# Two encoder layers on one core: the transposes of a head pair put in front of the value product of the pair before it

## What is computed

```python
def _L0_attn_ref(x, norm_scale, wq, wk, wv, w_out, b_out):
    h = _rmsnorm(x, norm_scale)
    q = jnp.einsum('bsd,dhe->bshe', h, wq)
    k = jnp.einsum('bsd,dhe->bshe', h, wk)
    v = jnp.einsum('bsd,dhe->bshe', h, wv)
    q = (q * head_dim ** -0.5)
    weights = jnp.einsum('bqhd,bkhd->bhqk', q, k)
    weights = jax.nn.softmax(weights, axis=-1)
    new_vals = jnp.einsum('bhqk,bkhd->bqhd', weights, v)
    return jnp.einsum('bqhe,hed->bqd', new_vals, w_out) + b_out
...
x = _layernorm(x + _L0_attn_ref(x, ...))
x = _layernorm(x + _L0_ffn_ref(x, ...))
x = _layernorm(x + _L1_attn_ref(x, ...))
x = _layernorm(x + _L1_ffn_ref(x, ...))
```

## Time and profile before

| | us |
|---|---|
| median of 3 runs | 1398.1 |
| lowest and highest of them | 1395.76, 1400.56 |
| the profiled execution | 1395.95 |
| its span, first to last instruction | 1394.2 |
| one turn, from OUT of turn 6 to OUT of turn 7 | 82.4 |
| TensorE busy over the span | 1329.1 |
| VectorE busy | 939.4 |
| ScalarE busy | 827.6 |
| GpSimd busy | 501.9 |

### The profile page before, as it was taken

One profiled execution on the slowest core, in us unless ns is written; L12 is line 12 of the kernel. 1 busy time (PEld: TensorE's weight loads), 2 busy tenths in 40 slices (PEclk: granted clock), 3 DMA queues, 4 the chain that ended last, 5 costly groups with the idle time before them and its releaser, 6 DMA issues.

```text
span 1394.2 us, 33724 instructions
## 1 busy us (share of the span) xinstructions
PE 1329.1 (95%) x11200; PEld 1177.8 (84%) x11200; DVE 939.4 (67%) x2663; ACT 827.6 (59%) x2236; POOL 501.9 (36%) x410
## 2 busy tenths in 40 slices
PE   6797999999999999999999999999999999999868
PEld 4575989899898988989898898989889898998758
DVE  5367576675767767676775757677676766757684
ACT  6564755657476574756657575665747556564423
POOL 3407062260705317071441706235070622607000
PEclk9999999999999999999999999999999999999988
DMA  6221000000000000000000000000000000000000
GB/s 186 58 63 33 9 22 12 21 18 12 19 11 23 11 19 11 19 19 8 26 12 15 15 15 23 8 23 15 15 16 14 21 11 20 14 12 21 5 0 9
DMA packets 39392, 30.90 MB, mean 22 GB/s; under 512 B 9897, under 2 KB 37426, under 8 KB 39346
## 3 DMA queue, kind: packets, MB, share of 16 engines
q1 hardware_dynamic: 39346, 30.33, 7.6%
HBM read 27.94 MB, written 2.36 MB: 22 GB/s over the span
## 4 chain that ended last, share of the span: by engine, by line
PE 80%; issue 8%; DVE 3%; POOL 3%; POOLq 2%; DVEq 1%; DMA 1%; SPq 1%; ACT 0%; ACTq 0%
PE bank_F L1222 22%; PE bank_S L1103 7%; PE bank_A L1159 7%; PE bank_T L1136 7%; PE bank_T L1089 4%; PE bank_A L1150 4%; PE bank_T L1090 3%; PE bank_T L1091 3%; PE bank_A L1089 3%; PE bank_F L1089 3%; PE bank_F L1091 3%; PE bank_F L1090 3%; PE bank_A L1091 3%; PE bank_A L1090 3%; POOLq L350 1%
## 5 line engine op out<-in xcount | busy, mean ns | idle before, releaser
L1222 PE MATMUL bank_F<-down,hid 128*128 128x128 f32 x2944 | 357.5, 277 | 5.4 <-DVE x L812 4.7
L1222 PEld LDWEIGHTS bank_F<-down,hid 128*128 128x128 f32 x2944 | 342.1, 193 | 14.4 <-DVE x L812 8.0
L605 ACT ACTIVATE probs<-bank_S,neg_max 128x256 f32<-128x256 f32 x512 | 235.7, 474 | 158.6 <-DVE neg_max L729 158.6
L729 DVE TENSOR_REDUCE neg_max<-bank_S 128x2 f32<-128x512 f32 x256 | 164.5, 684 | 77.2 <-PE bank_S L1103 77.1
L528 POOL TENSOR_TENSOR hid<-hid,qkv 128x1024 f32<-128x1024 f32 x60 | 169.0, 2827 | 11.3 <-ACT hid L621 11.3
L812 DVE SCALAR_TENSOR_TENSOR x<-bank_F,gates,x 128x128 f32<-128x128 f32 x496 | 149.5, 343 | 29.0 <-PE bank_F L1222 20.5
L589 ACT ACTIVATE probsT<-bank_T 128x512 f32<-128x512 f32 x256 | 138.9, 601 | 49.5 <-PE bank_T L1136 49.5
L498 POOL TENSOR_TENSOR mean_sq<-sum_sq,one_over_d 128x2 f32<-128x2 f32 x16 | 3.1, 196 | 429.5 <-ACT h_row L584 429.5
L1159 PE MATMUL bank_A<-probsT,values 128*64 128x256 f32 x1024 | 138.8, 392 | 9.0 <-DVE hid L746 4.1
L516 POOL TENSOR_TENSOR hid<-qkv 128x1024 f32<-128x1024 f32 x45 | 121.1, 2692 | 59.3 <-ACT qkv L589 59.3
L1136 PE MATMUL bank_T<-ident,probs 128*128 128x128 f32 x1024 | 137.5, 277 | 0.1
(11 more groups left out here) (184 smaller groups left out, 2896.3 us busy)
## 6 DMA issues: line engine op xcount, KB each, us to landing
inv_spread<-sums_apart SPq DMA_DIRECT2D x256, 64.0 KB, 2.6
sums_apart<-sum_invT SPq DMA_DIRECT2D x512, 0.5 KB
x_row<-in_x SPq DMA_DIRECT2D x16, 128.0 KB, 2.3
hid<-in_w SPq DMA_DIRECT2D x4, 512.0 KB, 4.5
down<-in_w SPq DMA_DIRECT2D x4, 512.0 KB, 4.4
out<-x SPq DMA_DIRECT2D x16, 128.0 KB, 1.8
hid<-in_rw SPq DMA_DIRECT2D x1, 1024.0 KB, 7.1
hid<-in_wv SPq DMA_DIRECT2D x1, 512.0 KB, 4.0
```

The costliest lines, as they stand in the source:

```text
L605: ins = sc.activation(probs[:, h // 2 % 2, h % 2, t, :], unit.bank(f"S{h}")[:, t * S:(t + 1) * S], ACT.Exp, bias=neg_max[:, h, t:t + 1], a ...
L729: ve.tensor_reduce(neg_max[:, h, :], v.bank(f"S{h}")[:, :].rearrange("p (t k) -> p t k", t=NT), AX.X, ALU.max, negate=True).then_inc(max_r ...
L1222: ins = te.matmul(bank[:, (j * NT + t) * P:(j * NT + t + 1) * P], hid[:, e, k, tokens(t)], down[:, e, k, :], start=k == 0, stop=k == m - 1)
```

## The change

In `pe_units` the line of O(s-1) moves from in front of the fill at place 0 and T(s) to behind them. In `transposed_probs` ScalarE gets a wait for O(s-1) in front of the copies of T(s), because that no longer follows from TensorE's order. The banks of all units stay the same, since O still stands in front of QK and HT in the ring of A0 and A1.

```diff
@@ -88,10 +88,10 @@
         put("A", "QK2", on=a and s == 0)
         put("S0", f"S{2 * s + 2}", on=a and s + 1 < HP)
         put("S1", f"S{2 * s + 3}", on=a and s + 1 < HP)
-        put("A", f"O{s - 1}", on=a and s >= 1)
         put("F", *fill_units(it, s, 0))
         put("T0", f"T{2 * s}", on=a)
         put("T1", f"T{2 * s + 1}", on=a)
+        put("A", f"O{s - 1}", on=a and s >= 1)
         put("A", f"QK{s + 3}", on=a and s + 3 < HP)
         put("A", "HT", on=nxt and s == HP - 2)
         put("F", *fill_units(it, s, 1))
@@ -652,6 +652,8 @@
             def transposed_probs(v, s):
+                if s >= 1:
+                    act.wait_ge(*v.fill(f"O{s - 1}"))
                 probsT_out(v, 2 * s)
                 probsT_out(v, 2 * s + 1)
```

## The result

The changed kernel takes 1420.49 us (median of four runs, 1418.06 to 1422.04), the kernel before 1399.33 on the same chip: a ratio of 1.0155, 95% interval 1.0132 to 1.0178, or about 21 us slower. The forecast was slower, by 11 us; its range ended at 1416. Run again on another chip the ratio was 1.0153 (1.0129 to 1.0177).

The account below looks back on a forecast made before the run. TensorE's own queue, busy 82.08 of 82.42 us per turn, was taken as the bound. Step terms sum to +0.79 us, 14 turns 11.1, first turns 0.5: +11.6, forecast 1409 us, range 1402 to 1416.

Parts of the forecast that it names:

- step 2: In a turn's step 2, T is followed by O, then QK; the extra layout change costs +0.18 us.
- step 3: X2T, now right behind S, waits about 0.4 us for VectorE's ln_apply; with the layout change +0.47 us.
- step 4: QK7 already waits for VectorE's lower_qk; the layout cost takes the place of that wait, 0 us.
- step 5: Work behind T is 16 fill matmuls; leaving to O and entering again cost +0.19 us.
- step 6: Work behind T is the two transposes HT; leaving to O and entering again cost +0.14 us.
- step 7: O6's wait for VectorE's o_scale goes, with no layout change added: -0.19 us.
- Cost 0: ScalarE's new wait for O makes copies late by 0.45 and some 0.7 us per turn, but cover hides it: 0.
- Turns 0 and 1: First two turns: TensorE waits for other engines there anyway, so 0.5 us, with bounds 0 and 1.6.
- X2T covered: Rival: ln_apply's chain runs ahead, X2T has no new wait; 0.41 us per turn, +6.2, 1404 us; chance 0.13.
- The layout change at no charge: Rival: TensorE loads O's weights while transposes run; 0.1 us per turn, +2, 1400 us; chance 0.07.
- O's waits worth more: Rival: hidden waits of O for copies and o_scale go in more steps; -2 us, 1396, faster; chance 0.05.
- ScalarE's wait reaching the path: Rival: ScalarE's delays reach S or the last T of a turn; +20 us, 1418; chance 0.13.

Follow-up runs that it names:

- late_turns: New order in turns 2 to 15 only, turns 0 and 1 as in the kernel before; 1415.29 us, ratio 1.0102 to the kernel before.
- after: The changed kernel's first profiled execution, whole change against the kernel before; this execution took 1422.04 us, the kernel's median 1420.49 us.
- first_turns: New order in turns 0 and 1 only, the order of the kernel before from turn 2 on; 1404.15 us, ratio 1.0036.
- x2t_steady: Changed kernel, but X2T stands behind T in step 3 of turns 2 to 14; 1411.44 us, ratio 1.0100 to the kernel before.
- x2t_behind: Changed kernel, but X2T stands behind T in step 3 of every turn; 1407.12 us, ratio 1.0056 to the kernel before.
- step7: Kernel before, with the new order in step 7 of turns 2 to 15 only; 1398.85 us, ratio 0.9997.
- step3_gate: Kernel before, new order in step 3 of turns 2 to 15, GpSimd's second head product held until VectorE's is done; 1408.36 us, ratio 1.0081.
- after_again: The changed kernel run once more, unaltered, on the chip of x2t_steady; 1419.95 us, ratio 1.0153 to the kernel before.

## Why the prediction was wrong, and where it was right

The forecast had 11.1 us for fourteen turns and 0.5 for the first two. In medians: 14 x 1.01 = 14.1 us of steady turns and 4.4 of the first turns are 18.5; the whole is 21.2. Of the remaining 2.7, late_turns shows 1.5 over its steady turns, as much as a part of the time behind OUT15 would give; the rest is within the measurement.

**The steps of a turn** held well, as the forecast's own list of signs had it. Between the S of one step and that of the next:

| part | forecast | measured |
|---|---|---|
| step 1 | 0 | 0.00 |
| step 2 | +0.18 | +0.20 |
| step 3 | +0.47 | +0.52 |
| step 4 | 0 | +0.01 |
| step 5 | +0.19 | +0.19 |
| step 6 | +0.14 | +0.15 |
| step 7 | -0.19 | -0.14 |
| OUT to the first S | 0 | +0.08 |
| turn | +0.79 | +1.01 |

T to O at 1.02, D0p3 and QK7 at their old distance to S, O6 without a wait, X2T about 1.3 us behind S with the idle time put to ln_apply: all as said. The chain of VectorE was costed rightly as far as ln_apply, which ends 1.23 us behind S, as forecast. The 0.06 us for its signal stood in no row: in after it is 0.15 us from the end of ln_apply (527.26) to X2T (527.41), 0.09 more; X2T itself, 0.24 instead of 0.28, gives 0.04 of that back, and the 0.05 left is the miss in step 3. The step that failed is what I left out behind it. "Cost 0" was argued for ScalarE's wait alone, and holds (no matmul waits for ScalarE in the steady turn, although ScalarE's idle time in front of its copies rose from 49.5 to 64.1 us). But VectorE, late by half a microsecond from X2T on, lost its place to GpSimd, and came late to OUT's second half and, as far as the distances tell, to the fills D1e3 and D1e4 in front of T: +0.08 and 0.05 in step 7. With the small misses of steps 2, 3, 4 and 6 that is 0.22 per turn, 3.1 us in all. In step 3 taken alone the same effect is 0.50 per turn; that it is small in the whole is step 5's and 6's doing, and for the forecast it was luck.

**Turns 0 and 1** were the larger failure: "TensorE there waits for the other engines anyway ... I take 0.5, since cover is plenty". They cost 4.4 in first_turns. The reading was upside down. TensorE's waits in turn 1 mean that a chain through ScalarE, VectorE and the matmuls sets the time; what TensorE does while it waits is free, but a unit that waits, put in front of a unit that didn't, puts the wait on everything behind it. The full turn's chain had been read to the hundredth, with VectorE only 0.4 us late for X2T; I never read the same stretch of turn 1, where X2T was already waiting 1.05 us with O2 in front of it. And turn 0, which has no X2T, isn't free either: at clock 1.00 throughout (x2t_steady against the kernel before), a QK waits 1.46 us there for lower_qk instead of 0.44, and a T 1.82 us for ScalarE where none did. Waits of O in front of T (up to 2.44 us in the kernel before) go in return, which is why only half a microsecond is left of it. The upper bound of 1.6 was taken from the steady turn, so the range couldn't hold it. How the 4.4 divide between these waits and the lower clock is open.

**Behind OUT15** the sum had no term. The profile shows 2.7 us at half clock; whether they belong to the change is open, as above.

**The rivals.** X2T covered: refuted, 0.40 us of wait in each steady turn. The layout change at no charge: refuted, T to O 1.02, and x2t_behind still costs 0.40 a turn. O's waits worth more: only step 7's, -0.18 in step7. (Its sum was wrong as well: without X2T's wait and with -0.19 twice more, the forecast's own terms give 0.41 - 0.38 = +0.03 a turn, about +1 us with the first turns, not -2.) ScalarE's wait reaching the path came nearest to the time (1418), for the wrong reason: no wait on ScalarE shows in a steady turn. The Trainium skill's rule that a change of tiling mode drains TensorE ("TensorEngine Tiling (Array Packing)", Key Properties) is borne out here with a price of 0.15 to 0.20 us for each extra pair of changes (0.20, 0.19 and 0.15 in steps 2, 5 and 6).

No version beat the kernel before by more than can be measured; step7 comes nearest.

## What to carry to other kernels

Ask of a unit that is moved forward in a full queue whether its input is there yet, and ask it in the ramp as well as in the steady turn: where an engine waits, the order of its queue decides what the wait falls on, and idle time there is no cover. Then follow a delay one engine further than the wait it causes: half a microsecond on VectorE changed which of two engines went first, and came back four steps later. And measure parts of a change singly only with care, since a delay that is hidden in the whole may show in the part, and the other way round.

## What the runs showed of the hardware

- Two 128x1024 products, one on VectorE and one on GpSimd, of 1.2 and 2.4 us alone, do not run side by side here: whichever starts 0.2 to 0.3 us earlier keeps nearly its time, and the other ends about when both would have ended one after the other (VectorE 1.34 and GpSimd 3.34, or 3.13 and 2.35; alone, in step3_gate, 1.20 and 2.36). A delay of 0.5 us on VectorE thus became one of 1.3 at neg_max.
- The granted clock of TensorE falls to 1.2 GHz for some microseconds at places that differ between profiles of the same kernel (in turn 1, 103 to 110 us in after, 105 to 109 in after_again), and from OUT0 to OUT2 those two profiles are 3.6 us apart (mean clock 0.92 and 0.95) with no change in the program. A difference of that size in one profile is no evidence; medians over several executions are.
